# float32r halves of q and k in four 32-row strips, and value matmuls issued for two steps at a time, in an attention and gated-MLP kernel

## What is computed

```python
qkv = jnp.einsum('bnc,cd->bnd', x, w_qkv).reshape(B, N, 3, NUM_HEADS, HEAD_DIM)
q, k, v = (qkv[:, :, 0], qkv[:, :, 1], qkv[:, :, 2])
q = _rmsnorm(q, q_scale)
k = _rmsnorm(k, k_scale)
q, k = _apply_rope(q, k)
q = q.astype(jnp.float32) * HEAD_DIM ** (-0.5)
logits = jnp.einsum('bqhd,bkhd->bhqk', q, k)
attn = jax.nn.softmax(logits, axis=-1)
out = jnp.einsum('bhqk,bkhd->bqhd', attn, v).reshape(B, N, C)
x = _layernorm(x + jnp.einsum('bnc,cd->bnd', out, w_proj) + b_proj)
h = jax.nn.silu(_tlin(x, w1_w, w1_s)) * _tlin(x, w2_w, w2_s)
h = jax.nn.gelu(_tlin(h, h1_w, h1_s), approximate=False)
h = jax.nn.gelu(_tlin(h, h2_w, h2_s), approximate=False)
x = _layernorm(x + _tlin(h, w3_w, w3_s))
```

## Time and profile before

| | us |
|---|---|
| median of 3 runs (416.61 to 416.75) | 416.7 |
| span of the profiled execution | 414.3 |
| its head, up to the first exponential | 42.2 |
| chunk 0, 64 exponentials | 64.4 |
| chunks 1 to 3, each | 89.2 |
| tail | 40.0 |

### The profile page before, as it was taken

One profiled execution on the slowest core, in us unless ns is written; L12 is line 12 of the kernel. 1 busy time (PEld: TensorE's weight loads), 2 busy tenths in 40 slices (PEclk: granted clock), 3 DMA queues, 4 the chain that ended last, 5 costly groups with the idle time before them and its releaser, 6 DMA issues.

```text
span 414.3 us, 6350 instructions
## 1 busy us (share of the span) xinstructions
PE 385.7 (93%) x2121; PEld 152.7 (37%) x2157; DVE 208.5 (50%) x397; ACT 315.4 (76%) x344; POOL 36.8 (9%) x27
## 2 busy tenths in 40 slices
PE   8985999999999999989999999999999999898992
PEld 3541222222233244533323353533332344433771
DVE  3899875010144645253344725254336543537755
ACT  2675999999888969597898868697889787881340
POOL 7042800000000000000000000001000000002001
PEclk9998999999999999999999999999999999999997
DMA  7997992403304040030403120301230400000000
GB/s 259 351 364 217 325 296 68 101 10 93 84 19 103 2 101 0 15 87 3 126 5 96 45 56 0 96 5 59 68 80 21 101 0 0 0 0 25 2 0 28
DMA packets 26933, 34.28 MB, mean 83 GB/s; under 512 B 1634, under 2 KB 19426, under 8 KB 26914
## 3 DMA queue, kind: packets, MB, share of 16 engines
q1 hardware_dynamic: 26674, 33.24, 28.1%
q0 software_dynamic: 240, 0.79, 0.5%
HBM read 20.98 MB, written 10.68 MB: 76 GB/s over the span
## 4 chain that ended last, share of the span: by engine, by line
PE 66%; ACT 16%; issue 8%; DVE 4%; DMA 3%; POOL 2%; ACTq 0%; SPq 0%; POOLq 0%; DVEq 0%
PE ps L450 21%; PE ps L460 20%; ACT probs L742 10%; PE ps L519 9%; PE ps L599 4%; PE ps L509 3%; ACT ffn L753 2%; ACT L753 2%; DMA va<-v_all 2%; PE ps L425 2%; PE ps L477 1%; DVE g_hi L898 1%; POOL parts L390 1%; PE ps L653 1%; ACT L742 1%
## 5 line engine op out<-in xcount | busy, mean ns | idle before, releaser
L742 ACT ACTIVATE probs<-ps 128x1024 f32<-128x1024 f32 x256 | 247.5, 1023 | 51.9 <-PE ps L450 51.3
L450 PE MATMUL ps<-qa,ka 128*128 128x512 bf16 x478 | 132.2, 382 | 8.6 <-ACT probs L742 3.6
L460 PE MATMUL ps<-probs,va 128*9 128x512 f32 x1024 | 131.1, 594 | 2.1 <-ACT probs L742 1.9
L450 PEld LDWEIGHTS ps<-qa,ka 128*128 128x128 bf16 x512 | 38.7, 98 | 112.3 <-ACT probs L742 63.2
L928 DVE TENSOR_SCALAR ffn<-ps,col 128x512 f32<-128x512 f32 x36 | 27.0, 750 | 68.6 <-PE ps L519 52.6
L519 PE MATMUL ps<-g_hi,w_hi 128*128 128x512 f32 x108 | 46.7, 433 | 2.4 <-DVE ffn L928 2.4
L519 PE MATMUL ps<-g_lo,w_hi 128*128 128x512 f32 x108 | 42.4, 393 | 0.0
L460 PEld LDWEIGHTS ps<-probs,va 128*9 128x9 f32 x1024 | 16.8, 88 | 60.5 <-issue 37.4
L397 POOL TENSOR_TENSOR rs<-ve,mhalf 128x4 f32<-128x4 f32 x6 | 6.1, 1017 | 309.5 <-DVE ve L887 309.5
L866 DVE COPY oT<-ps 128x512 f32<-128x512 f32 x15 | 10.4, 692 | 32.3 <-PE ps L460 32.3
L899 DVE TENSOR_TENSOR g_lo<-ffn,g_hi 128x512 fp32r<-128x512 f32 x36 | 24.9, 692 | 1.2
(11 more groups left out here) (118 smaller groups left out, 332.7 us busy)
## 6 DMA issues: line engine op xcount, KB each, us to landing
ka<-k_scr SPq DMA_DIRECT2D x16, 576.0 KB
qa<-q_scr SPq DMA_DIRECT2D x16, 288.0 KB
q_scr<-parts SPq DMA_DIRECT2D x9, 384.0 KB, 6.3
k_scr<-parts SPq DMA_DIRECT2D x9, 384.0 KB, 5.2
va<-v_all SPq DMA_DIRECT2D x16, 144.0 KB
ffn<-in_h SPq DMA_DIRECT2D x2, 1024.0 KB, 8.7
q_scr<-rope SPq DMA_DIRECT2D x3, 384.0 KB, 5.8
k_scr<-rope SPq DMA_DIRECT2D x3, 384.0 KB, 5.8
```

The lines of the kernel that those rows point to most:

```text
L450: mm = pe.matmul(s_tile(u)[:, i, :], ka[:, slot, h, kt * P:(kt + 1) * P], qa[:, slot, h, :], start=True, stop=True)
L460: mm = pe.matmul(ps[32 * h:32 * h + VW, O_BANK, :], va[:, g % 2, kt, h, :], probs[:, step % 4, h, :], start=(kt == 0), stop=(kt == KT - 1))
L742: nc.scalar.activation(probs[:, step % 4, 2 * pair:2 * pair + 2, :], s_tile(u), ACT.Exp).then_inc(exp_done, 1)
```

## The change

Each of q and k is split into two float32r halves (`PARTS` 2) instead of three bf16 parts. `QROWS` becomes 2 x 2 x 8 = 32 rows for a head, so the four heads of a group fill the 128 partitions, head j in rows 32j to 32j+31. A logits matmul reads only the 32 rows of its head. The third part, POOL's subtraction, the 48-row zero stores, the memsets of the spare rows and the row-maximum load of the normal case are gone; POOL instead sets `ones_k`, which only the case with row maxima reads (`shifted`). `HELD_STEPS` holds the even steps 2 to 30 of chunks 1 to 3, so an odd step issues the values of two steps. The stores are 512 KB each, two for a half; the loads are 512 KB for `ka` and 256 KB for `qa`. The chunk bodies exist in more forms, of which one runs.

```diff
-PARTS = 3
+PARTS = 2
 QROWS = PARTS * PARTS * HD
-HELD_STEPS = (19, 20, 25, 28, 30)
+HELD_STEPS = tuple(range(2, STEPS, 2))
...
-        ka = sb("ka", [KROWS, 2, HG, SEQ], BF16)
-        qa = sb("qa", [KROWS, 2, HG, CH], BF16)
+        ka = sb("ka", [P, 2, SEQ], F32R)
+        qa = sb("qa", [P, 2, CH], F32R)
+        qm = sb("qm", [P, 2, CH], BF16)
...
-                sp.dma_start(dst[0:QROWS], scr[bass.ds(HG * QROWS * g, HG * QROWS), bass.ds(t0, count)].rearrange("(h r) t -> r h t", h=HG)).then_inc(signal, 16)
+                sp.dma_start(dst.bitcast(F32), scr[bass.ds(HG * QROWS * g, HG * QROWS), bass.ds(t0, count)]).then_inc(signal, 16)
...
-                pool.tensor_tensor(parts_of(t)[:, 2, :], res, parts_of(t)[:, 1, :], ALU.subtract).then_inc(p3_done, 1)
...
                 for i in range(2):
-                    h = 2 * pair + i
-                    mm = pe.matmul(s_tile(u)[:, i, :], ka[:, slot, h, kt * P:(kt + 1) * P], qa[:, slot, h, :], start=True, stop=True)
+                    rows = slice(32 * (2 * pair + i), 32 * (2 * pair + i) + QROWS)
+                    mm = pe.matmul(s_tile(u)[:, i, :], ka[rows, slot, kt * P:(kt + 1) * P], qa[rows, slot, :], start=True, stop=not shifted)
...
-                    act.wait_ge(res_done, t + 1)
-                    nc.scalar.copy(parts_of(t)[:, 1, :], res).then_inc(p2_done, 1)
...
-            def residue(t):
+            def low_part(t):
...
+                dve.wait_ge(p1_done, t + 1)
+                nc.vector.tensor_tensor(parts_of(t)[:, 1, :], hn, parts_of(t)[:, 0, :].bitcast(F32), ALU.subtract).then_inc(p2_done, 1)
...
-            residue(NCH - 1)
-            dve.wait_ge(res_done, NCH)
-            nc.vector.tensor_copy(last[:, 1, :], res).then_inc(last_parts, 1)
+            nc.vector.tensor_tensor(last[:, 1, :], hn, last[:, 0, :].bitcast(F32), ALU.subtract).then_inc(last_parts, 1)
```

More of the change, by code:

```diff
@@ L149, in build @@
         W2K = 2 * CH
-        sq, lnv, rinv, rot_a, rot_b, hn, res = (prep[:, i * W2K:(i + 1) * W2K] for i in range(7))
+        sq, lnv, rinv, rot_a, rot_b, hn = (prep[:, i * W2K:(i + 1) * W2K] for i in range(6))
         MT = HG * KT
@@ L322, in load_for_max, with later_loads @@
                     load_rows(qa[:, i], q_scr, g, b * SEQ + i * CH, CH, max_in)
+            def later_loads(shifted):
+                sp.wait_ge(v_evac, 4)
+                sp.wait_ge(scr_out[0], 2 * STORED)
+                sp.wait_ge(scr_out[1], 2 * STORED)
+                with sp.Fori(1, NCH) as c:
+                    for g in range(NG):
+                        load_group(c, g, shifted=shifted)
             store_parts(0)
@@ L437, in prepare, with logits @@
                 mm.then_inc(var_ready, 1)
-            def logits(c, step, pair):
+            def logits(c, step, pair, shifted):
                 g, kt = divmod(step, KT)
@@ L558, in chunk @@
                 for step in range(STEPS):
-                    logits(c, step, 0)
+                    logits(c, step, 0, shifted)
                     if passes:
                         ffn_at(base, c - 1, 2 * step, passes)
-                    logits(c, step, 1)
+                    logits(c, step, 1, shifted)
                     if step == 1 and not passes:
@@ L684, in _ @@
                 pe.wait_ge(max_rows, BATCH * NG)
-            chunk(0, 0)
+                pe.wait_ge(ones_set, 1)
+                chunk(0, 0, True)
+            with pe.If(wide == 0):
+                chunk(0, 0, False)
             pe.wait_ge(lo_flag, 1)
-            low = pe.value_load(flags_i[0:1, 1:2], min_val=0, max_val=1)
-            with pe.If(low == 0):
-                later_chunks(2)
-            with pe.If(low == 1):
-                later_chunks(4)
+            form = pe.value_load(flags_i[0:1, 1:2], min_val=0, max_val=2)
+            with pe.If(form == 0):
+                later_chunks(2, False)
+            with pe.If(form == 1):
+                later_chunks(4, False)
+            with pe.If(form == 2):
+                later_chunks(4, True)
         @block.scalar
@@ L715, in _ @@
                 if t:
[L716 to L718 removed]
+                    high_part(t - 1)
                 act.wait_ge(var_ready, t + 1)
```

147 lines of the change are left out of this document (59 added, 88 removed).

## The result

The changed kernel took **442.3 us** (median of 4 runs, 441.1 to 443.0) against 416.7 for the one before: 1.061 times as long, 95% interval 1.059 to 1.063. It is slower by 25.7 us; the prediction was 390.6.

The account below looks back on a forecast made before the run. PE was taken to pace chunk 0 and most of the later chunks, with ACT's 1.84 us step as floor. Span 414.3 - 4.5 (head) - 3.3 (chunk 0) - 18.3 (chunks 1 to 3) = 388.2, plus 2.4 outside: 390.6 us; range 378 to 411.

Parts of the forecast that it names:

- Strips that overlap: Logits on PE: a pair's two matmuls run at once in their strips, 0.28 us alone, 0.25 behind another pair.
- (a): Rival, all 256 pairs: strips do not overlap, a pair takes 0.46 us, kernel slower at 426.5 us; chance 0.14.
- (b): Rival, strip pairs: the second strip's weight load cannot overlap, a pair takes 0.41 us, kernel 416.6 us; chance 0.12.
- Head: Up to the first exponential: earlier store and shorter load bring it at 37.7 instead of 42.2 us, -4.5.
- Chunks 1 to 3: Later chunks, summed over five stretches: 83.2 instead of 89.3 us each, -18.3 in all.
- A: Steps 0 to 7 of a later chunk: 15.8 us instead of 17.9, with small ACT stalls at projection and transposes.
- B: Steps 8 to 16, with an `up` each: PE still sets the pace, 20.7 us instead of 22.2.
- C: Steps 17 to 20, four `hidden` up to the Gelu: no gain, 16.7 us against 16.2.
- D: Steps 21 to 25: 17.8 us instead of 19.2, the Gelu waiting for the fourth `hidden` behind two sets of values.
- E: Steps 26 to 31: 12.2 us instead of 13.8, with `down` and the last transposes delaying ACT.
- The held steps: Chunks 1 to 3: holding values at every even step saves ten changes of form, 2.4 us of PE a chunk.
- Rival (c): Chunk 0: PE's thinner work lets its clock fall, at least +20 us, about 420 us; chance 0.04.

Follow-up runs that it names:

- e13: Changed kernel with the old five held steps, GpSimd's residual add late, and TensorE's unused forms nested behind the taken path; 405.8 us.
- e5: Changed kernel with GpSimd's residual add late and the used form of chunk 0 put first in TensorE's program; 440.8 us.
- e1: Changed kernel with the five held steps of the kernel before (19, 20, 25, 28, 30); 414.8 us.
- e15: e13 with every even step from 2 held, as the change has it; 433.1 us.
- e2: Kernel before (bf16, 128 rows) with only the held steps changed, to every even step from 2; 436.7 us.

## Why the prediction was wrong

**Strips that overlap: right, and priced nearly right.** The price was the question on which I put most weight, and rivals (a) and (b) were both wrong: two pairs in a row cost 0.44. For the changed kernel's double `up` step I had forecast 4.5. It is 4.93, and 0.47 of that is no price of a strip. The three places of pairs take 1.28 for 1.45 forecast, the two `up`s 1.34 for 1.22, the values 1.84 for 1.83. What was missing is the wait of the second `up` for the perceptron's one bank, 0.47: I had counted this wait for `hidden` and not for `up`, and it is there because the values that stood between the two are held. With the old list, where every pair in these steps is alone, two such steps take 5.0 (2 x 2.50), 0.2 more than before: what a strip pair is worth depends on the list.

**Chunk 0: right in mechanism, 0.9 off.** ACT's distance is 0.92 with no idle time within a group of 24, and e13 takes 62.0 against 61.1 predicted (64.4 before). In the changed kernel it took 62.8; from 43 to 54 us the clock was granted at 0.53.

**Head: within its bounds, but on the wrong kernel.** -4.5 was predicted, with bounds of -1.5 (if the DMA queue alone decides) and -6; the kernels from e5 on have -1.5 to -4.7, e13 -4.6, and the long ones are those in which PE waits for `va`. In the changed kernel it is +3.4. The term lacked two things. One is GpSimd: I took its subtractions away and did not ask what stands behind them in its queue. The residual add moved 30 us forward and met the one DVE instruction that all wait for. The other is in no engine's timeline: TensorE had to step over a whole chunk of unused code while the DMA engines were full. "The change adds a form" was in the diff and cost nothing in my sum.

**Chunks 1 to 3: wrong, -18.3 predicted, +21.8 measured.** With the old list they give -7.4 (e13). The forecast was for the new list, so the changed kernel's chunk 1 is its measure (B cut at the fourth Tanh, as the earlier trace rows have it): A 17.2 for 15.8, B 24.4 for 20.7, C 17.1 for 16.7, D 22.4 for 17.8, E 16.1 for 12.2. Only C is near. Even with the old list no stretch but C comes below its forecast (e13, chunk 2: 16.8, 21.4, 15.9, 19.4 and 14.3, and 12.8 for E in chunk 1, where the clock held).

**The held steps: the step that decided.** I wrote "Holding values at every even step saves ten changes there and back, 2.4 us of PE a chunk", and that exponentials wait for values four steps older, "enough". The first can't be seen: PE is busy for 84.5 us in chunk 1, against 82.8 in e1 with the old list, partly at half its clock. A saving would have been worth little, as PE then waits. The second looks at the wrong wait. No exponential waited for a `probs` buffer, that is for values. What waited: DVE's copy of a finished group and behind it, in DVE's queue, the pre-activation of ACT's next Tanh or Gelu; the next group's values behind the same copy; the second `up` and the bank that it needs; and ACT, because a set of two with the projection behind it is longer (2.9) than the two tiles that it lives on (1.84). The term put at -2.4 a chunk is +9.1 by the medians (e15 against e13, 27.3 over three chunks). I had written that "three PSUM tiles let PE be ahead by 2.8 us at most" and still did not go through every set with it.

**Rival (c), the clock: the right mechanism at the wrong place.** I priced it at 0.04 and in chunk 0, from PE's thin work. It fell behind the Gelu blocks and in the first 10 us of chunk 0. Its share is some 1.5 us a stretch where it strikes, by the estimate above about a third of the list's loss. It's not the main part: e2 loses 5.9 us in a chunk at 1.00 throughout.

**Tail: 0 predicted, +1.5 measured,** all of it behind the last matmul (8.2 for 6.7 us), where TensorE steps over one branch more and two more packets of instructions come. That these fetches are the cause is inferred.

## What to carry to other kernels

Packing matmuls into strips pays where strips stand next to strips: price a pair with its entry and its exit, and count the isolated ones first. Before work is given later (held, bunched), list what stands *behind* each waiter in its own engine's queue and compare the longest stretch without fresh input with the buffers that the consumer has; busy time saved on an engine that then waits buys nothing. When work is removed from an engine, ask what moves up in its queue, and keep rarely taken code out of the way of the taken path, above all where the DMA engines are full.
